# Taking the row minimum of the audio scores in two pieces instead of one

## The reference

```
a = layer_norm(audio_kv); Q = x @ Wq.T; K = a @ Wk.T; V = a @ Wv.T   # 16 heads of 16
scores = einsum('bhtd,bhsd->bhts', Q, K) * scale                     # 8 x 16 x 56 x 1500
scores = where(mask, scores, -inf)
attn = softmax(scores, axis=-1)
out = (attn @ V) @ Wo.T
x = x + tanh(gate) * out
```

## Time and profile before

| | us |
|---|---|
| median of 3 runs | 1448.81 (1448.06 to 1450.09) |
| the profiled execution | 1447.18 |
| its span, first to last instruction | 1445.4 |
| audio tiles, y = 0 to 55, in that span | about 1126 to 1430 |
| matmul busy over the span | 1384.9 |
| VectorE busy over the span | 987.6 |
| ScalarE busy over the span | 855.7 |

### The profile page before, as it was taken

The page is one execution under the profiler, slowest core; times in us unless marked ns, Lnnn a source line. Parts: engine busy times, 40 slices in busy tenths (PEclk is TensorE's granted clock), DMA queues, the critical chain, the costliest instruction groups (busy, mean ns, idle before and its releaser), DMA issues.

```text
span 1445.4 us, 29611 instructions
## 1 busy us (share of the span) xinstructions
PE 1384.9 (96%) x11632; PEld 854.1 (59%) x11632; DVE 987.6 (68%) x2031; ACT 855.7 (59%) x1505; POOL 478.2 (33%) x393
## 2 busy tenths in 40 slices
PE   9999999999999999999999999999999999889966
PEld 5466666666666655566666666666554444444434
DVE  6865555555555658877566566565658899889975
ACT  6655545445455447645544544545545799889974
POOL 5545434434334200234533522520002344334300
PEclk9999999999999999999999999999999999999998
DMA  6399988889898820599988989988622799999998
GB/s 214 91 233 195 189 166 185 179 170 180 181 169 179 164 97 30 114 219 192 189 168 181 182 167 179 186 167 153 181 56 61 129 208 207 211 207 209 198 181 149
DMA packets 652934, 242.62 MB, mean 168 GB/s; under 512 B 625548, under 2 KB 627068, under 8 KB 652796
## 3 DMA queue, kind: packets, MB, share of 16 engines
q1 hardware_dynamic: 652796, 240.73, 83.1%
HBM read 85.28 MB, written 0.52 MB: 59 GB/s over the span
## 4 chain that ended last, share of the span: by engine, by line
PE 76%; DVE 10%; DMA 5%; issue 4%; ACT 4%; SPq 2%; ACTq 0%; POOL 0%; DVEq 0%; POOLq 0%
PE SC L828 41%; PE PV L828 34%; DMA core<-qc 3%; DVE qc L1707 3%; DVE prob L1689 3%; DVE core L1748 2%; ACT qc L1420 1%; DMA core<-core 1%; ACT core L1395 1%; DMA core<-in_wv_dram 1%; ACT rowbuf L1438 0%; DVE core L1740 0%; SPq L597 0%; ACT prob L1411 0%; SPq L599 0%
## 5 line engine op out<-in xcount | busy, mean ns | idle before, releaser
L828 PE MATMUL PV<-core 128*128 128x256 f16 (+1 forms) x7104 | 492.6, 238 | 24.8 <-ACT small L1426 11.8
L828 PEld LDWEIGHTS PV<-core 128*128 128x128 f16 (+1 forms) x7104 | 414.5, 96 | 91.8 <-ACT small L1426 14.8
L1340 ACT ACTIVATE prob<-SC,core 128x500 f32<-128x500 f32 x336 | 223.8, 675 | 409.4 <-DVE core L1713 408.7
L828 PE MATMUL SC<-ctxT,qc 128*128 128x500 f16 x2016 | 443.4, 374 | 0.0
L1682 DVE TENSOR_REDUCE mx<-SC 128x1 f32<-128x500 f32 x330 | 220.9, 669 | 313.1 <-PE SC L828 313.1
L828 PEld LDWEIGHTS SC<-ctxT,qc 128*128 128x128 f16 x2016 | 196.0, 97 | 206.8
L756 POOL CAST ctxT<-stage 128x750 f16<-128x750 f32 x64 | 67.4, 1053 | 428.1 <-PE SC L828 224.2
L1740 DVE SCALAR_TENSOR_TENSOR core<-prob,core 128x1500 f16<-128x1500 f32 x112 | 201.3, 1797 | 6.4 <-ACT core L1349 6.3
L1349 ACT ACTIVATE core<-prob 128x1500 f16<-128x1500 f32 x112 | 162.7, 1453 | 3.5
L828 PE MATMUL SC<-ctxT 128*128 128x512 f16 x552 | 134.8, 383 | 4.4 <-DVE core L1748 4.3
L828 PE MATMUL SC<-qc 128*128 128x512 f16 x480 | 118.9, 394 | 19.6 <-DVE mx L1689 17.1
(11 more groups left out here) (151 smaller groups left out, 1352.1 us busy)
## 6 DMA issues: line engine op xcount, KB each, us to landing
stage<-in_ctx_nat_dram SPq DMA_DIRECT2D x64, 384.0 KB, 3.9
stage<-in_ctx_t_dram SPq DMA_DIRECT2D x64, 375.0 KB, 3.4
stage<-in_ctx_p_dram SPq DMA_DIRECT2D x32, 384.0 KB, 4.1
core<-in_wq_dram SPq DMA_DIRECT2D x8, 512.0 KB, 3.5
core<-in_wk_dram SPq DMA_DIRECT2D x8, 512.0 KB, 3.5
core<-in_wv_dram SPq DMA_DIRECT2D x8, 512.0 KB, 5.0
core<-in_wo_dram SPq DMA_DIRECT2D x8, 512.0 KB, 5.0
core<-core SPq DMA_TRANSPOSE x224, 4.0
```

Of the source, the lines that this page charges most:

```text
L828: return nc.tensor.matmul(o, a, c, start=start, stop=stop, skip_group_check=skip)
L1340: nc.scalar.activation(prob[:, i, c * CW:c * CW + w], SETS[i][c][:, 0:w], ACT.Exp, bias=nmax[:, i, :], accum_out=sum3[:, i, c:c + 1]).then ...
```

## The change

The single minimum instruction becomes two: the front piece covers the first two banks (1024 columns), the rear piece the third bank (476 columns). Each has a semaphore from TensorE that starts it (`as_front` after bank 1, `as_score` after bank 2) and one that it raises (`front_max`, `rear_max`). Their two minima go to columns 0 and 1 of `mx3`; a `tensor_tensor` of one element per row joins them in column 2 and raises `as_max`, which ScalarE's exponential waits for. TensorE starts the first two banks of the next tile after `front_max`, and the third after `rear_max`.

```diff
@@ audio_scores(y), TensorE
                 if y == 0:
                     pe.wait_ge(m_lo, PRE_UNITS)
                 else:
-                    pe.wait_ge(as_max, y)
+                    pe.wait_ge(front_max, y)
                 for c in range(NB):
                     at = c * 512
+                    if c == NB - 1 and y > 0:
+                        pe.wait_ge(rear_max, y)
...
+                    if c == NB - 2:
+                        ins.then_inc(as_front, 1)
                 ins.then_inc(as_score, 1)
@@ audio_exponentiate(y), ScalarE
-                nc.scalar.activation(prob[:, i, 0:T], prob[:, i, 0:T], ACT.Exp, scale=-1.0, bias=mx3[:, i, 0:1],
+                nc.scalar.activation(prob[:, i, 0:T], prob[:, i, 0:T], ACT.Exp, scale=-1.0, bias=mx3[:, i, 2:3],
@@ audio_minimum(y), VectorE
-                dve.wait_ge(as_score, y + 1)
-                nc.vector.tensor_tensor_reduce(
-                    out=prob[:, i, 0:T], in0=scores_of(y), in1=maskb[:, b % 2, :], scale=1.0, scalar=3.0e38,
-                    op0=ALU.add, op1=ALU.min, accum_out=mx3[:, i, 0:1]).then_inc(as_max, 1)
+                front = (NB - 1) * 512
+                for k, (lo, hi) in enumerate(((0, front), (front, T))):
+                    dve.wait_ge((as_front, as_score)[k], y + 1)
+                    nc.vector.tensor_tensor_reduce(
+                        out=prob[:, i, lo:hi], in0=scores_of(y)[:, lo:hi], in1=maskb[:, b % 2, lo:hi], scale=1.0,
+                        scalar=3.0e38, op0=ALU.add, op1=ALU.min, accum_out=mx3[:, i, k:k + 1])\
+                        .then_inc((front_max, rear_max)[k], 1)
+                dve.wait_ge(front_max, y + 1)
+                dve.wait_ge(rear_max, y + 1)
+                nc.vector.tensor_tensor(mx3[:, i, 2:3], mx3[:, i, 0:1], mx3[:, i, 1:2], ALU.min).then_inc(as_max, 1)
```

More of the change, by code:

```diff
@@ L250, in build @@
         as_max = sem("as_max")
+        as_front = sem("as_front")
+        front_max = sem("front_max")
+        rear_max = sem("rear_max")
         as_exp = sem("as_exp")
```

## The result

| | kernel before | changed kernel |
|---|---|---|
| median of 14 runs each | 1448.02 us | 1452.30 us |
| the profiled execution | 1447.18 | 1453.51 |
| its span | 1445.4 | 1451.7 |
| start of the first to start of the last minimum of the stage | 300.57 | 303.57 |

The ratio of the two is 1.0023, with a 95% interval from 1.0013 to 1.0034. That is some 3.3 us slower (1.9 to 4.9; the two medians are 4.3 apart), a little more than the 2.9 us that were called the least one can tell, though the interval holds those 2.9. The forecast of 1450.0 (+1.2) was too low by some 2 us.

The account below looks back on a forecast made before the run. No engine has room: of 38 us per batch element TensorE is busy 35.98, VectorE 34.31, ScalarE 32.70. A price of +8.1 less gains at waiting tiles gave +1.2, on a 1448.8 median 1450.0 us; range 1444.0 to 1455.5.

Parts of the forecast that it names:

- likeliest case: Whole kernel: costs and gains cancel, time within some 2.9 us of before, 1447.0 to 1452; 45%.
- the price: VectorE, each split minimum: two pieces and dependent join delay what follows by 0.27 us a tile.
- tiles s = 3: Five tiles s = 3 that waited for scores: -0.38 us each over three tiles, -1.9 together; y = 31 taken as -0.4.
- tile 21: Minimum 21, which waited 1.50 us for six matmuls: split ends it at T + 1.19 instead of T + 1.66, -0.5 us.
- How many tiles pay: 30 tiles pay the 0.27 us: 7 in batch element 0, 20 of y = 7 to 46, 3 at the end; +8.1 us.
- The last ten tiles: Last batch element, TensorE starting 0.50 us earlier: y = 47 and 50 -1.4 each, y = 52 -0.9, y = 54 -0.4.
- y = 47: Tile 47, said to have the same form as y = 50: 0.50 us earlier and 0.87 less from T to E, -1.4.
- Rival D: Transposes really pace batch elements 1 to 6, so 20 tiles' 5.4 us vanish and gains stay: -4.2 us, 1444.6; 11%.
- Rival B: TensorE's clock falls in more batch elements after a pick gap 0.27 us longer: +1.3 us each, 1451.3 to 1456.7; 16%.
- A2: VectorE: each instruction waits for the one before to end, losing 0.08 us overlap in the pieces: +3.6, 1452.4; 7%.
- A: VectorE: each piece costs its whole length, price 0.42 us, deciding from 0.33 on: +5.7, 1454.5; 12%.
- C: Loop at the end: TensorE's clock stays higher as gaps shrink, speeding y = 47, 50, 52: -4.1 on the forecast, 1445.9; 9%.

Follow-up runs that it names:

- light transposes: Low transpose of each tile carries only its first half of the tokens, the average using stale values; ratios 0.9926 on the kernel before, 1.0016 on the changed kernel.
- light kernel before: Kernel before with the low transpose of each tile carrying only its first half; 1438.13 us, ratio 0.9926 to the kernel before.
- price alone: Changed kernel without early signals: TensorE waits for the join, both pieces for the last bank; 1456.27 us, ratio 1.0052; with halved low transposes 1454.36, 1.0042.
- kernel with the early start only: Kernel before with tiles 46 to 55 in two pieces, front started on its own signal, TensorE waiting for the join; 1448.97 us, ratio 0.9995.
- changed light kernel: Changed kernel with the low transpose of each tile carrying only its first half; 1451.30 us, ratio 1.0016 to the kernel before.
- ten-tile split: Kernel before with two pieces and early signals only for tiles 46 to 55; 1447.15 us, ratio 0.9988.
- four-tile split: Kernel before with two pieces and early signals only for tiles 49, 50, 52 and 53; 1445.85 us, ratio 0.9984.
- one-wait version: Changed kernel with halved low transposes and no wait for the front's minimum ahead of the join; 1445.94 us, ratio 0.9982 to the kernel before.

## Why the prediction was right or wrong

**The call.** The range held; the likeliest case, no change that can be told, did not: +3.3 is just beyond it. That the sum of +1.2 came within some 2 us was luck. It was too low by the price (1.8 in the five quiet stretches) and by the tiles s = 3 (1.7), and too high by tile 21 (0.9) and the end (0.4). But the gains at tile 21, in tile 31 and at the end were this large only because the kernel before has its three long steps there, and the sum had no term for what makes them: with light transposes, where they are missing, the same change costs 13.2 us.

**The price, 0.27 us a tile.** This step failed in size. "The join waits for that: a small instruction that depends on the one before starts 0.04 after its end" is right for one wait; the diff has two, and the forecast read it as one. With both the price is 0.37, with one 0.28 (S + 1.91). At 0.10 on each of 30 tiles that is 3.0 us, more than the whole miss. The pieces themselves, and the exponential that is late by the same amount (1255.32, E + 0.09), were right.

**How many tiles pay.** Right for the stretches without a wait: 5 x 1.44 = 7.2 us is the price on four tiles each, 0.36 a tile.

**Tiles s = 3.** -2.3 forecast, -0.6 measured, and the -0.6 is no real gain: against the light kernel before, five of the six stretches became 0.3 to 0.4 longer and the sixth 1.6, and the difference is -0.6 only because three in before (17.18, 17.14, and 19.06 around tile 31) held more waiting than that. The -0.4 taken for y = 31 failed by its source: minimum 31 waits 1.28 us in the light kernel before, and the other 2.5 of the 3.76 were a transpose that held ScalarE up and the lower clock behind it. The step from T to E that was said to be 1.01 took 1.60 in tile 17 (1224.45 to 1226.05), of which 0.35 is the wait for ScalarE. The sum had asked where the front's start goes and not what stands behind the join.

**Tile 21.** -0.5 forecast; it lost 2.35 of its step (8.66 to 6.31). The wait for a transpose ahead of it was 2.21 us instead of 3.28, and the six matmuls of its scores took 1.97 instead of 2.77. With light transposes in the changed kernel no such wait stands there and the step is 5.78.

**The last ten tiles.** -3.3 with the price of three of them, -3.7 measured. TensorE's start at 1.37 and the step to y = 54 were right. y = 50 gave -1.75 and y = 52 -0.98 (forecast -1.4 and -0.9). y = 47 gave -2.19 for -1.4, but not by the mechanism: it does not have "the same form" as y = 50. Its 2.48 us of the earlier trace rows came from the hole of 2.21 us inside its scores shown above, which the changed kernel's profile does not have; the light kernel before, without the hole, has a step of 5.78 there, and the changed kernel 6.16. That the number was near was luck.

**Rival D** had 11% and is the largest effect of the case, though not as it was put. It said that transposes would swallow the price of 20 tiles, 5.4 us, and the time would fall. But the quiet tiles paid in full, with full transposes and with light ones. What went were long steps of the kernel before, three of them above all, in the lines that the forecast had booked as gains of the split. Together that took some 10 us off the change's cost (13.2 less 3.3), and the price was itself larger. The row that I dismissed it by, 3.1 us of ScalarE's waiting, was one of three: TensorE's 4.9 and VectorE's 1.8 stood beside it, and the wait at 1237.47 shown above cost TensorE its clock too.

**Rival B** came about once: after the pick gap ahead of tile 45 TensorE ran slower, and the stretch from s = 1 took 18.13 instead of 16.90. That is 1.2 us against the 1.3 worked out. It is no rare chance. In the profiles of the five kernels that have both signals in all tiles it came in 10 of 30 batch elements, and in those of the price alone (full and light) and of the light kernel before in none of 18, at gaps of nearly the same length (1.34 to 1.42). The gap 0.27 longer that was to bring it about did not come (1.38 in the light kernel before, 1.41 to 1.42 in the changed one); what the early signals have to do with it is not shown. **A2** did not happen: the overlap of 0.08 between the pieces stayed (1253.23 to 1254.37 is 1.14 for a piece of 1.22). The Trainium skill, "VectorE: DVE Perf Modes", section "The DRAIN you can't avoid", makes an exception to the rule that the forecast cited: an instruction that is not held starts earlier. The 0.08 agrees with the exception, not with the rule. The forecast's estimate of 0.35 by that rule came nearer to 0.37 than mine, by another cause: the missing part sits ahead of the join. **A** fell as a mechanism, since the pieces overlap, and its 0.42 is over the 0.37; but 0.37 is over the 0.33 from which it was said to decide, and the time did go where it pointed. **C** is not seen in the changed kernel: the twelve matmuls of y = 50 still take 4.44. It is seen in others at the same place: y = 50 took 2.75 in the kernel with the early start only, and y = 52 took 2.76 in the changed light kernel, the ten-tile split and the four-tile split.

**Left open:** why the waits for transposes fade when VectorE is slower. Of the 9.8 us that the three engines waited for them in the kernel before, 4.1 are left in the changed kernel, 0.6 in the price alone, and none up to y = 55 in the changed light kernel; that shows what they hang on, not the order of events on the queue. What the holes in TensorE's work are, and whether they hang on the transposes. And which half of the split earns the gain at the end.

## What to carry to other kernels

Count the waits ahead of an instruction, not only the instructions: when one engine raises two signals in order, wait for the last alone (here worth 3 to 5 us of 1450). Split an instruction for an early signal only at the tiles whose rows show another engine waiting for it, and look at what stands behind the join, for it may already be late from elsewhere. When a trace holds waits on a third party (here transposes), make that party lighter in an experiment before and after: it shows how much of a change's cost is hidden by delays that only the faster kernel meets, which here was 10 of 13 us. And before a wait is booked as a gain, look at what the engine waited for itself was doing: three waits for scores here were two transposes and a hole.

## What the runs showed of the hardware

A semaphore wait that is long satisfied, ahead of one that is not, cost 0.09 to 0.10 us on VectorE (join 0.11 after the read's end and the next instruction 0.10 after its start, against 0.04 and 0.08 with one wait).

A reduction that takes its start value from a result of just before started 0.14 us after that result's read, with two waits ahead of it, and lasted 0.71 instead of 0.65.

The length of a gap alone does not settle what TensorE's clock does. TensorE in the changed kernel, after a gap of 1.41 us in tile 17, and after the same gap ahead of tile 45:

```profile
1219.48 0.98 PE L831 MATMUL PV<-core 128*32 128x56 f16 x96 [1.41 <-ACT small L1433]
...
1378.41 1.08 PE L831 MATMUL PV<-core 128*32 128x56 f16 x96 [1.41 <-ACT small L1433]
1379.43 2.42 PE L831 MATMUL SC<-ctxT 128*128 128x512 f16 x6
1381.65 3.52 PE L831 MATMUL SC<-qc 128*128 128x512 f16 x12
```

After the first the twelve matmuls of the scores took 2.75, all at the higher level (granted clock 1.00 in 1219.48 to 1224.50); after the second 3.52, and six matmuls of a unit 2.42 instead of 1.46 (0.75 in 1378.41 to 1385.20). In the changed kernel with light transposes the gap ahead of tile 45 was 1.42, and there the unit took 1.47. At y = 52 the twelve matmuls took 2.76 after a gap of 2.44 in the changed light kernel, and 4.45 after one of 2.36 in its one-wait version. The forecast had read a gap of 1.97 as safe and one of 2.27 as not; the runs don't bear such a bound out. What decides is open.
